# One 256-column score product for the first plain and the first latent tile in heads two to four, with the first half of the next latent keys made in slot 4 of the second pass

## What is computed

```
q = rope(x @ w_q);  k = rope(x @ w_k);  v = x @ w_v            # 32 heads of q, 8 of k and v
lq = x @ w_lq                                                  # 1024 x 128
lk = rope(lq @ w_lk);  lv = x @ w_lv                           # 32 heads each
attn = causal_attn(q, repeat(k, 4), repeat(v, 4), SCALE)
lat  = causal_attn(q, lk, lv, SCALE)
x = x + attn @ w_o + lat @ w_lo                                # x was layer-normed first
x = x + ffn(layernorm(x))                                      # with a routed low-rank part
```

## Time and profile before

| | |
|---|---|
| runs | 2035.51, 2036.35, 2037.13 us; median 2036.35 |
| the profiled execution's own time | 2036.75 us |
| its span in the trace | 2035.0 us, so 1.75 us lie around it |
| PE busy | 2018.2 us, 99% |
| DVE, ACT, POOL busy | 1457.1, 1203.7, 889.9 us |
| mean granted TensorE clock | 0.998 of 2.4 GHz |

### The profile page before, as it was taken

How to read it: one execution, slowest core, us unless ns; L and a number is a source line. 1 busy time by engine, 2 the same in 40 slices (tenths; PEclk the granted TensorE clock), 3 DMA queues, 4 the chain that set the end, 5 groups by cost and what they waited for, 6 DMA issues and landing times.

```text
span 2035.0 us, 33416 instructions
## 1 busy us (share of the span) xinstructions
PE 2018.2 (99%) x11716; PEld 1753.1 (86%) x11716; DVE 1457.1 (72%) x2884; ACT 1203.7 (59%) x2505; POOL 889.9 (44%) x684
## 2 busy tenths in 40 slices
PE   8999999999999999999999999999999999999989
PEld 7888888888888888888888888888888888888877
DVE  7677776776777767777677776777776776777777
ACT  4666556565565656666566565666566565565651
POOL 5444544444443454444534454444544444443422
PEclk9999999999999999999999999999999999999999
DMA  3111111111111111112111111111111111111031
GB/s 108 47 34 44 48 28 38 34 49 37 38 39 39 33 44 37 44 28 49 33 44 37 39 39 28 49 34 44 48 28 41 32 49 39 37 39 38 23 68 42
DMA packets 101797, 83.78 MB, mean 41 GB/s; under 512 B 28152, under 2 KB 73848, under 8 KB 101632
## 3 DMA queue, kind: packets, MB, share of 16 engines
q1 hardware_dynamic: 101632, 81.65, 15.7%
HBM read 79.26 MB, written 2.36 MB: 40 GB/s over the span
## 4 chain that ended last, share of the span: by engine, by line
PE 97%; DVE 2%; ACT 1%; POOL 0%; issue 0%; DMA 0%; DVEq 0%; ACTq 0%
PE bankT L587 13%; PE scores L514 12%; PE scores L516 12%; PE scores L515 12%; PE bankX L514 9%; PE bankX L516 9%; PE bankX L515 9%; PE bankO L516 7%; PE bankO L515 7%; PE bankO L514 7%; PE scores L707 0%; PE scores L553 0%; DVE rot_half L1124 0%; DVE xnT_lo L1097 0%; ACT probs L876 0%
## 5 line engine op out<-in xcount | busy, mean ns | idle before, releaser
L815 ACT ACTIVATE PT_hi<-bankT 128x512 fp32r<-128x512 f32 (+2 forms) x640 | 337.5, 533 | 310.7 <-PE bankO L516 275.5
L1113 DVE TENSOR_TENSOR PT_lo<-bankT,PT_hi 128x512 fp32r<-128x512 f32 (+2 forms) x640 | 388.1, 607 | 175.7 <-ACT PT_hi L815 173.1
L876 ACT ACTIVATE probs<-probs,nmax 128x128 f32<-128x128 f32 (+7 forms) x512 | 393.9, 771 | 129.8 <-DVE nmax L1107 129.7
L1107 DVE CUSTOM_DVE_ANT_0 probs<-scores,mask 128x128 f32<-128x128 f32 (+7 forms) x512 | 379.2, 750 | 69.3 <-PE scores L516 68.0
L587 PE MATMUL bankT<-ident,probs 128*128 128x128 f32 x2304 | 382.7, 275 | 6.8 <-ACT probs L876 5.0
L587 PEld LDWEIGHTS bankT<-ident,probs 128*128 128x128 f32 x2304 | 279.6, 140 | 67.9 <-DVE PT_lo L1113 11.7
L1369 POOL TENSOR_TENSOR rot<-rot,cos 128x512 f32<-128x512 f32 x144 | 186.9, 1298 | 256.6 <-DVE rot_half L1124 256.6
L1363 POOL TENSOR_TENSOR OT_lo<-o_raw,OT_hi 128x512 fp32r<-128x512 f32 x63 | 98.3, 1560 | 319.9 <-ACT OT_hi L815 319.9
L815 ACT ACTIVATE OT_hi<-o_raw 128x512 fp32r<-128x512 f32 x128 | 146.7, 1146 | 139.7 <-DVE o_raw L1182 139.7
L1371 POOL TENSOR_TENSOR rot<-rot,rot_half 128x512 f32<-128x512 f32 x144 | 199.9, 1388 | 11.3
L1123 DVE TENSOR_TENSOR rot_half<-rot,sin 64x512 f32<-64x512 f32 x144 | 99.5, 691 | 135.3 <-ACT rot L815 132.3
(11 more groups left out here) (304 smaller groups left out, 5334.0 us busy)
## 6 DMA issues: line engine op xcount, KB each, us to landing
inv_b<-inverses SPq DMA_DIRECT2D x128, 256.0 KB, 3.9
stage<-in_L_attn_w_q SPq DMA_DIRECT2D x32, 256.0 KB, 4.8
stage<-in_L_attn_w_lv SPq DMA_DIRECT2D x32, 256.0 KB, 2.9
stage<-in_L_attn_w_o SPq DMA_DIRECT2D x32, 256.0 KB, 3.5
stage<-in_L_attn_w_lo SPq DMA_DIRECT2D x32, 256.0 KB, 2.6
acc<-in_L_attn_hidden_states SPq DMA_DIRECT2D x8, 256.0 KB, 4.9
stage<-in_L_attn_w_k SPq DMA_DIRECT2D x8, 256.0 KB, 5.0
stage<-in_L_attn_w_v SPq DMA_DIRECT2D x8, 256.0 KB, 5.0
```

What stands on the lines that cost most here:

```text
L815: return act.activation(place, src, ACT.Copy)
L876: act.activation(prob_tile(c, t), prob_tile(c, t), ACT.Exp, bias=nmax[:, c, t:t + 1], scale=-1.0, accum_out=rsum[:, c, t:t + 1]).then_inc( ...
L1107: dve.tensor_tensor_reduce(place, src, tile_view(mask[:, S - width:S], c), -SCALE, -MASKED, ALU.add, ALU.min, nmax[:, c, t:t + 1]).then_in ...
L1113: dve.tensor_tensor(pt_place(1, hh, w, j), bankT[j % 2][:, block_columns(c, j):CH], f32(pt_place(0, hh, w, j)), ALU.subtract).then_inc(pt_ ...
```

## The change

The plain and the latent keys now lie in one pair of tensors `keys_T` (`KT` and `LKT` are its two halves). For hh = 1 to 3 the first tile of w = 0 and the first tile of w = 2 are one product with the same 128 queries, of 2 x 128 columns, in slot 4 of w = 3 of the head before; DVE's `row_max` and ACT's exponential still run once for each, the latent one into a tensor of its own (`probs_ahead`) until w = 2. The latent tile in slot 1 of w = 1 is gone for these heads. So that the keys are there in time, ("LK", 0) of the next head becomes ("LKA", 0), in slot 4 of w = 1 of the head before, and no longer stands in slot 0 of w = 0. The weights Wlk are loaded earlier: ACT's copy in slot 2 of w = 1 (slot 5 for hh = 3) in place of slot 5 of w = 3. ACT's `rope_high` of LKA stands in slot 0 of w = 2 behind Wo, with a wait until all tiles of w = 3 were scored; POOL's `rope_low` of it stands between the low parts of Wo and Wlo. `row_max` and `exp_tile` take their place in the order from `tiles_at` and their number from a table; the order within a slot is as before.

```diff
--- before.py
+++ after.py
-        return {0: ("LK", 0), 1: ("LK", 1), **({3: ("LV", 0)} if more else {})}
+        return {**({0: ("LK", 0)} if hh == 0 else {}), 1: ("LK", 1), **({3: ("LV", 0)} if more else {})}
     if w == 1:
         if (g, hh) == FIRST:
-            return {0: ("LV", 1), 2: ("LV", 2), 5: ("LV", 3)}
+            return {0: ("LV", 1), 2: ("LV", 2), 4: ("LKA", 0), 5: ("LV", 3)}
         out = {s: ("OUT1", n) for n, s in enumerate((1, 2, 4, 7) if next_group else (1, 3, 5, 7))}
         ahead = {3: ("K", 0), 5: ("K", 1), 6: ("V", 0)} if next_group else {}
-        return {**({0: ("LV", 1)} if more else {}), **out, **ahead}
+        latent = {4: ("LKA", 0)} if hh < GROUP - 1 else {}
+        return {**({0: ("LV", 1)} if more else {}), **out, **ahead, **latent}
     if w == 2:
...
-        return (["Wk", "Wv"] if hh == GROUP - 1 else []) + ["Wq", "Wo", "Wlo", "Wlk"]
+        return (["Wk", "Wv"] if hh == GROUP - 1 else []) + ["Wq", "Wlk", "Wo", "Wlo"]
     if (g, hh) == (KVH - 1, GROUP - 2):
-        return ["Wq", "Wo", "Wlo", "Wlk"]
-    return ["Wq", "Wlv0", "Wo", "Wlo", "Wlk", "Wlv1"]
-
...
+def tiles_at(g, hh, w, s):
+
+    if w == NW - 1 and (g, hh) == FINAL:
+        return []
+    to = (g, hh, w + 1) if w < NW - 1 else (*divmod(g * GROUP + hh + 1, GROUP), 0)
+    tiles = []
+    for t in range(TPC):
+        if TILE_SLOTS[w][t] == s:
+            if t or w != 1 or hh == 0:
+                tiles.append((*to, t))
+            if t == 0 and w == NW - 1 and to[1]:
+                tiles.append((*to[:2], 2, 0))
+    return tiles
+
...
+        keys_T = pair("keys_T", [P, 2, S])
...
+        probs_ahead = sb("probs_ahead", [P, P])
...
+            return 2 if w == 2 else WINDOWS[w][1]
...
+            return probs_ahead[:, :] if (w, t) == (2, 0) else prob_tile(WINDOWS[w][1], t)
...
-                            fetch("Wq", "Wlv0" if "Wlv0" in loads_of(g, hh) else "Wo")
+                            fetch("Wq", "Wlk")
...
-                    if hh == GROUP - 1 or "Wlv0" in loads_of(g, hh):
-                        fetch("Wo")
-                    fetch("Wlo")
+                    if hh == GROUP - 1:
+                        fetch("Wlk")
+                    if "Wlv0" in loads_of(g, hh):
+                        fetch("Wlv0")
+                    fetch("Wo", "Wlo")
                     spread_inverses(g, hh, 2)
-                    fetch("Wlk")
...
+                kind, c = WINDOWS[w]
+                parity, head = t % 2, hh
+                if AHEAD_IN_SCORES[g, hh, w, t]:
+                    pe.wait_ge(row_maxed, TILE_NO[AHEAD_IN_SCORES[g, hh, w, t]] + 1)
...
+                if (w, t) == (0, 0) and hh:
+                    mm3(scores[0][:, 0, 0:2 * P].rearrange("p (k n) -> p k n", k=2), query,
+                        both(keys_T, ALL, ALL, slice(0, P)), True, True).then_inc(scored, 2)
+                    return
...
+                elif name == "LKA":
+                    pe.wait_ge(w_lo, load_no(g, hh, "Wlk") + 1)
+                    mm = mm3(banksX[bank], both(Wlk, ALL, ALL), both(lqT, ALL, slice(0, CH)), True, True)
...
+                        for at in tiles_at(g, hh, w, s):
+                            t = at[3]
+                            if w == 3 and at[2] == 2:
+                                continue
+                            if t == 0 and w == 1:
+
+                                pe.wait_ge(rope_lo, rope_no(g, hh, "LK", 0) + 1)
+                            if t == 0 and w == 2:
+
+                                pe.wait_ge(rope_lo, rope_no(g, hh, "LK", 1) + 1)
+                            if t == 0 and w == 3:
+
+                                pe.wait_ge(rope_lo, rope_no(g, hh, "Q", 0) + 1)
+                            if t == 0 and w == 0:
+
+                                pe.wait_ge(rope_lo, rope_no(g, hh, "LK", 1 if hh else 0))
+                            if t == 1 and w == 0:
+                                pe.wait_ge(x_free, frees_ahead(g, hh, 0))
+                            if t == 1 and w == 2:
+                                pe.wait_ge(x_free, frees_ahead(g, hh, 2))
+                            score_tile(*at)
...
-                        if name in ("Q", "K"):
+                        for at in tiles_at(g, hh, w, s):
+                            exp_tile(*at)
+                        if name in ("Q", "K", "LKA"):
...
+                        if w == 1 and s == (5 if hh == GROUP - 1 else 2) and more:
+                            act.wait_ge(x_ready, n_piece(g, hh, 0, 1))
+                            fetched(g, hh, "Wlk", Wlk)
...
-                        if w == 3 and s == 5 and more:
-                            fetched(g, hh, "Wlk", Wlk)
+                            if s == 0 and hh < GROUP - 1:
+                                act.wait_ge(scored, tiles_made(g, hh, 3))
+                                rope_high(rope_no(g, hh, "LKA", 0), rope_no(g, hh, "LKA", 0) % RING, LKT[0][:, 0:CH])
...
+                first = P if (w, t) == (2, 0) and hh else 0
+                place = tile_view(tile_of(w, t), c)
+                src = scores[parity][:, 0, first:first + width] if c == 0 else scores[parity][:, :, 0:width // 2]
...
-                        if here.get(s - 1, ("", 0))[0] == "LK":
+                        if here.get(s - 1, ("", 0))[0] in ("LK", "LKA"):
...
+                halves = range(1 if hh and name == "LK" else 0, 2)
...
+                        if hh < GROUP - 1:
+                            fetched_low(g, hh, "Wlk", Wlk)
                     if w == 1 and k_no:
...
+                            rope_add(rope_no(g, hh, "LKA", 0), rope_no(g, hh, "LKA", 0) % RING, 0)
...
+                            rope_low(rope_no(g, hh, "LKA", 0), rope_no(g, hh, "LKA", 0) % RING, LKT, (ALL, chunk(0)))
```

More of the change, by code:

```diff
@@ L81, in loads_of, with number_tiles @@
     if hh % 2:
-        return (["Wk", "Wv"] if hh == GROUP - 1 else []) + ["Wq", "Wo", "Wlo", "Wlk"]
+        return (["Wk", "Wv"] if hh == GROUP - 1 else []) + ["Wq", "Wlk", "Wo", "Wlo"]
     if (g, hh) == (KVH - 1, GROUP - 2):
-        return ["Wq", "Wo", "Wlo", "Wlk"]
-    return ["Wq", "Wlv0", "Wo", "Wlo", "Wlk", "Wlv1"]
-ROPE = ("Q", "K", "LK")
+        return ["Wq", "Wlk", "Wo", "Wlo"]
+    return ["Wq", "Wlk", "Wlv0", "Wo", "Wlo", "Wlv1"]
+def tiles_at(g, hh, w, s):
[10 more added lines that the diff above has]
+    return tiles
+def number_tiles():
+    order = [(*FIRST, 0, t) for t in range(TPC)]
+    for g in range(KVH):
+        for hh in range(GROUP):
+            for w in range(NW):
+                for s in range(BLOCKS[w]):
+                    order += tiles_at(g, hh, w, s)
+    last, ahead = [None, None], {}
+    for at in order:
+        ahead[at] = last[at[3] % 2]
+        last[at[3] % 2] = at
+    return {at: no for no, at in enumerate(order)}, ahead
+TILE_NO, AHEAD_IN_SCORES = number_tiles()
+ROPE = ("Q", "K", "LK", "LKA")
 X_BEFORE = 10
@@ L239, in attn_ffn_kernel @@
         Wlv0, Wlv1 = [[h[:, :, k * HD:(k + 1) * HD] for h in Wlv] for k in range(2)]
+        KT, LKT = [[h[:, kind, :] for h in keys_T] for kind in range(2)]
         f32 = lambda ap: ap.bitcast(F32)
@@ L560, in out_tile, with score_tile @@
                 return mm3(banksX[bank], both(OT, ALL, 1, rows), both(Wlo, ALL, ALL), False, True)
-            def score_tile(no, parity, head, kind, c, t):
-                if not (isinstance(no, int) and no < 2):
-                    pe.wait_ge(row_maxed, no - 1)
+            def score_tile(g, hh, w, t):
+                kind, c = WINDOWS[w]
+                parity, head = t % 2, hh
+                if AHEAD_IN_SCORES[g, hh, w, t]:
+                    pe.wait_ge(row_maxed, TILE_NO[AHEAD_IN_SCORES[g, hh, w, t]] + 1)
                 i = TPC * c + t
@@ L887, in block_hi @@
                 copy(pt_place(0, hh, w, j), bankT[j % 2][:, block_columns(c, j):CH]).then_inc(pt_hi, 1)
-            highs = [{(0, 3): ("LK", 0), (1, 0): ("LK", 1), (3, 1): ("Q", 0), (3, 3): ("Q", 1)} for _ in range(GROUP)]
+            highs = [{(0, 3): ("LK", 0), (1, 0): ("LK", 1), (3, 1): ("Q", 0), (3, 3): ("Q", 1)}
+                     for _ in range(GROUP)]
             highs[GROUP - 1].update({(1, 5): ("K", 0), (2, 0): ("K", 1)})
@@ L901, in group_of_heads @@
                                       piece_bank(g, hh, w, s))
-                        early = s + 2 < BLOCKS[w] and name in ("", "LK", "OUT0", "OUT1")
+                        early = s + 2 < BLOCKS[w] and name in ("", "LK", "LKA", "OUT0", "OUT1")
                         if early:
                             block_hi(g, hh, w, s + 2)
-                        if more or w < NW - 1:
-                            for t in range(TPC):
-                                if TILE_SLOTS[w][t] == s:
-                                    exp_tile(tiles_made(g, hh, w) + t, WINDOWS[nw][1], t)
-                        if name in ("Q", "K"):
+                        for at in tiles_at(g, hh, w, s):
+                            exp_tile(*at)
+                        if name in ("Q", "K", "LKA"):
```

(22 more changed lines are left out.)

70 lines of the change are left out of this document (26 added, 44 removed).

## The result

| kernel | median, us | runs | ratio to before, 95% interval |
|---|---|---|---|
| before | 2036.74 | 4 | |
| changed | 2102.68 (2099.97 to 2104.81) | 4 | 1.0323 [1.0307, 1.0338] |

What follows compares the result with a forecast made beforehand. PE, busy 2018.2 of 2035.0 us, was taken as the bound. Terms -7.6 - 4.3 + 14.6 + 31.1 + 9.6 = +43.4 us on 2036.75 gave 2079.8 by the median, taken as 2078; range 2052 to 2088.

Steps and rivals of the forecast that it cites:

- Term 1: Slot 4 of w = 3: three 256-column matmuls replace six of 128, 0.32 us less a head, -7.6 us.
- Term 2: Slot 1 of w = 1: PE's wait for the latent keys' low part goes in hh = 1 to 3, -4.3 us.
- Term 3: Slot 0 of w = 0: without its LK piece, the first product waits for DVE to empty bankO, +14.6 us.
- Term 4: Slot 5 of w = 1: LKA's two DVE multiplications ahead of row_max of tile 3 make PE wait, +31.1 us.
- Term 5: Slot 0 of w = 2: LKA's high part on ACT delays Wlo_lo and DVE's chain to the output product, +9.6 us.
- The waits are half as large: Rival, chance 0.2: DVE and POOL do not hold each other up, Term 4 and Term 5 at low ends; 2062 us.
- More: Rival, chance 0.1: Wlv0's DMA lands late in w = 1 and holds ACT; 2090 us and above.
- faster: Rival, chance 0.07: the chains of Term 3 and Term 4 have cover, leaving only Term 1 and Term 2; 2024 us.

Runs made afterwards that it cites:

- the control: The kernel before, with POOL's low part of the queries' first half waiting for DVE's multiplications for the second half: 2036.73 us, 1.0001.
- the two other repairs: Changed kernel, DVE order rewritten, plus POOL's QT_lo waiting for DVE's second-half multiplications and ("LK", 1) in slot 0 of w = 0 for hh = 1 to 3: 2033.42 us.

## Why the prediction was right or wrong

**Term 1 (-7.6): right.** 6.6 us measured by the time, 7.4 by the length of the slot.

**Term 2 (-4.3): its mechanism was right.** 8 waits are left of 32. No run takes it alone. By the lengths, slots 0 and 1 of w = 1 are 0.50 us shorter in these heads; 3 x 0.112 = 0.34 of it are the matmuls of the tile that is gone, so the wait was 0.16 us a head, 3.9 in all.

**Term 3 (+14.6): right.** The first product of w = 0 waits for o_raw, as these lines of the changed kernel show (hh = 2; compare):

```profile
424.95 0.47 PE L559 MATMUL bankO<-PT_hi,V_lo 128*128 128x512 f32 x1 [0.25 <-DVE o_raw L1242]
```

```profile
424.13 0.68 DVE L1242 TENSOR_TENSOR o_raw<-bankO,inv_b 128x512 f32<-128x512 f32 x1
```

From o_raw's start to the product are 0.82 us, 0.84 before: DVE's chain did not get shorter, so moving the piece out gained nothing here. The lag is 0.68 us a head where 0.61 was forecast: the product starts 0.14 us after o_raw's end, and the forecast had 0.08.

**Term 4 (+31.1): right, in both kinds of heads.** The last slot of w = 1 lags by 1.68 us in heads with Wlv0 (forecast 1.65) and 0.75 in those without (0.7). The collision with Wlv_lo took place, but only the first multiplication paid for it:

```profile
449.98 1.29 POOL L1421 TENSOR_TENSOR Wlv_lo<-stage,Wlv_hi 128x512 fp32r<-128x512 f32 x1 [4.78 <-ACT Wlv_hi L870]
```

```profile
450.42 1.39 DVE L1183 TENSOR_TENSOR rot_half<-rot,sin 64x512 f32<-64x512 f32 x1
451.82 0.68 DVE L1184 TENSOR_TENSOR rot_half<-rot,sin 64x512 f32<-64x512 f32 x1
```

Taken back, it gave 36.5 us by the medians, 33.3 by the length of the slot.

**Term 5 (+9.6) is the step that failed.** It was priced as "0.4 us later, x 24": one delay, handed on along the chain o_raw, OT_hi, OT_lo. Measured are a lag of 0.19 us in slot 1 of w = 3 in all 24 heads, less than the 0.4 (Wlo's low part came 0.29 us later and not 0.5), and 1.28 against 0.17 in slot 2 in the 23 heads that lost the race: 4.6 + 25.5 = 30 us, 20 more than forecast. The 25.5 are the failure. The extra is no delay handed on. It is a change of order between two engines that want the same way to SBUF, which the earlier trace rows did not reach: they end before POOL's QT_lo at 453.77. The start of DVE's second multiplication, 0.15 us ahead of it, stood in the trace of the kernel before and was not read. That the order makes the loss is shown by the two runs that set it by force, one each way (-23.6 and +49.4), and that the wait is no gain of its own by the control (0.0). That the small delay comes from the collision on Wlo's low part is shown by the run that removes it. That this delay alone turned the order is argued from the starts, since that run made POOL later too. The prediction's upper bound for this term was 12.

**The sum.** With the measured sizes it is -6.6 - 3.9 + 16.3 + 33.6 + 30.1 = +69.5 (term 4 as 15 x 1.75 + 9 x 0.82, counted from the -0.07 of that slot in the kernel before). The profiled executions, which the lags are read from, lie 2104.81 - 2036.75 = 68.1 apart; the 66 are between the medians, and the profiled execution of the changed kernel was the slowest of four. So to about 1.5 us each delay was lost for good, as the prediction counted it; the 1.8 us that it took off its sum (2079.8 to 2078) had no ground in the rows.

**The rivals.** "The waits are half as large" took DVE and POOL not to hold each other up; they do. "More" was given 0.1 and was the right case by its time, but that is luck, for its mechanism was another: no DMA of Wlv0 was late for PE, and its page shows no DMA on the chain. The rival "faster" named a fixed order on DVE as the thing against it; with that order rewritten, and the two other repairs, the kernel is 0.17% faster than before, where its terms 1 and 2 had promised 12 us. Of the 9 that are missing the lags show 7.4: 0.17 us a head (4 us) still go in slot 1 of w = 3 behind Wlo's low part, and 0.14 (3.4 us) in slot 3 of w = 0.

## What to carry to other kernels

When a moved instruction makes a neighbour even 0.2 us later, look in the trace for every pair of DVE and GpSimd instructions on two SBUF tensors behind it that start within that distance of each other, and ask who would win; a delay that is absorbed can still turn a pair around, and the loser pays nearly the whole of the other's instruction (1.1 of 1.28 us here). Where the loser must not be the engine that TensorE waits for, a semaphore wait on the other engine fixes the order, and costs nothing if that engine has time; but it moves that engine's next work, so follow it to the end. A line's mean duration can stay the same while its long cases move to where they hurt: look at the long ones by place, not at the mean.

## What the runs showed of the hardware

- In a collision of DVE and POOL on SBUF tensors the one that started first ran at its own pace. In the race of the fourth pass, over the three traces in which it is open, a lead of POOL of 0.012 us or more was enough in every head; in the seven heads in which its start is recorded 0.004 or 0.005 us ahead, DVE won. When POOL led, DVE's multiplication (64 x 512) ended 0.54 to 0.55 us after POOL's instruction, however early it had started: 471.90 + 1.80 against 471.88 + 1.28; 450.42 + 1.39 against 449.98 + 1.29; 465.23 + 0.89 against 464.29 + 1.28. So a late overlap is cheap and an early one dear, up to 1.1 us on 0.69. When DVE led in the race, POOL's subtraction ended 1.15 us after DVE's (453.77 + 1.69 against 453.62 + 0.69). This is the lock on a shared port that the Trainium skill describes (SBUF — State Buffer, Terms): held for the whole instruction, while the loser fully blocks. The trace agrees but for 0.14 us: in these pairs the loser ends that much earlier than if it had begun only at the other's end (0.55 after it, not 0.69; 1.15, not 1.29).
- The outcome is not the same in every head of one execution: 23 of 24 heads lost the race in the changed kernel, and 18 with a piece moved in another pass. Lags worked out for one head are therefore good for the sum only with a count.
